# Ten sums of a codebook level go behind the block sums of the queries' stage

## The reference, cut to what matters

```python
def _L0_attn_ref(hidden_states, Wq, bq, Wk, bk, Wv, bv, Wo, bo, gq, gk):
    q = rms_norm(hidden_states @ Wq + bq, gq)      # 32 heads x 128, keys alike
    attn = softmax(einsum('bhqd,bhkd->bhqk', q, k) * scale)
    out = einsum('bhqk,bhkd->bhqd', attn, v)
    return out @ Wo + bo

def _L0_cond2_ref(x, weight, scale_log, codebook, lora_A, lora_B):
    lora_delta = lora_B @ lora_A * (LORA_ALPHA / LORA_RANK)
    cb = codebook / clip(max(abs(codebook)), 1e-08)
    normalized = (weight + lora_delta).reshape(O, I // GROUP, GROUP) / exp(scale_log)
    idx = searchsorted((cb[:-1] + cb[1:]) * 0.5, normalized, side='left')
    w = cb[idx] - normalized + normalized
    return x @ ((w * scale).reshape(O, I) + lora_delta).T
```

## Time and profile before

| what | value |
|---|---|
| median of 3 runs | 1450.33 us |
| the profiled execution | 1451.06 us |
| its span, first to last instruction | 1449.3 us |
| TensorE matmuls busy | 1444.4 us (100%) |
| TensorE weight loads busy | 1200.5 us (83%) |
| VectorE busy | 1080.4 us (75%) |
| ScalarE / GpSimd busy | 726.0 us (50%) / 745.2 us (51%) |
| granted TensorE clock | 1.000 |

### The profile page before, as it was taken

One profiled execution on the slowest core, in us unless ns is written; L12 is line 12 of the kernel. 1 busy time (PEld: TensorE's weight loads), 2 busy tenths in 40 slices (PEclk: granted clock), 3 DMA queues, 4 the chain that ended last, 5 costly groups with the idle time before them and its releaser, 6 DMA issues.

```text
span 1449.3 us, 34721 instructions
## 1 busy us (share of the span) xinstructions
PE 1444.4 (100%) x14507; PEld 1200.5 (83%) x14507; DVE 1080.4 (75%) x1507; ACT 726.0 (50%) x1331; POOL 745.2 (51%) x530
## 2 busy tenths in 40 slices
PE   9999999999999999999999999999999999999999
PEld 8788888888888888888888888888888888888887
DVE  8787868687786877875478888867987667667663
ACT  7766676766766767677333333334432322222221
POOL 7568777777777877776345555514561111112100
PEclk9999999999999999999999999999999999999999
DMA  4211011110111011102443344447663334244230
GB/s 152 66 45 45 31 38 45 45 45 24 45 45 45 27 41 45 45 31 67 136 152 139 133 133 137 145 148 246 201 194 110 103 118 132 83 137 132 74 118 30
DMA packets 106989, 135.13 MB, mean 93 GB/s; under 512 B 6224, under 2 KB 89424, under 8 KB 106320
## 3 DMA queue, kind: packets, MB, share of 16 engines
q1 hardware_dynamic: 106400, 132.62, 27.7%
q10 hardware_dynamic: 432, 0.30, 0.1%
HBM read 86.75 MB, written 46.14 MB: 92 GB/s over the span
## 4 chain that ended last, share of the span: by engine, by line
PE 98%; DVE 1%; issue 0%; ACT 0%; DVEq 0%; POOL 0%; ACTq 0%; POOLq 0%
PE bank L720 41%; PE bank L963 25%; PE bank L739 21%; PE bank L922 4%; PE bank L848 3%; PE bank L991 1%; PE bank L1009 1%; PE bank L669 0%; DVE wa L1623 0%; PE bank L648 0%; PE bank L977 0%; PE bank L1020 0%; DVE xs_lo L1685 0%; DVE sqst L1707 0%; PE bank L1041 0%
## 5 line engine op out<-in xcount | busy, mean ns | idle before, releaser
L720 PE MATMUL bank<-xs_hi,wa 128*128 128x512 f32 x1792 | 563.9, 392 | 0.0
L1526 POOL TENSOR_TENSOR accr<-accr,sqst 128x512 f32<-128x512 f32 x248 | 351.9, 1429 | 149.7 <-ACT sqst L1196 109.9
L720 PEld LDWEIGHTS bank<-xs_hi,wa 128*128 128x128 f32 x1792 | 336.3, 188 | 74.5 <-DVE qk L1774 2.4
L720 PE MATMUL bank<-xs_lo,wa 128*128 128x512 f32 x896 | 349.0, 390 | 0.0
L963 PE MATMUL bank<-ot,wo_main 128*128 128x512 f32 x1344 | 316.4, 392 | 0.0
L963 PEld LDWEIGHTS bank<-ot,wo_main 128*128 128x128 f32 x1344 | 249.6, 188 | 52.5
L739 PE MATMUL bank<-wv,xs_hi 128*128 128x512 f32 (+1 forms) x1008 | 282.6, 366 | 0.1
L1623 DVE TENSOR_TENSOR wa<-wraw,wa 128x256 fp32r<-128x256 f32 (+1 forms) x160 | 159.4, 997 | 96.2 <-ACT wa L1105 94.3
L1321 ACT ACTIVATE ot<-bank,vec 128x256 fp32r<-128x256 f32 x256 | 100.2, 475 | 240.4 <-PE bank L963 146.5
L739 PEld LDWEIGHTS bank<-wv,xs_hi 128*128 128x128 f32 x1008 | 182.1, 189 | 32.8 <-issue 1.9
L720 PEld LDWEIGHTS bank<-xs_lo,wa 128*128 128x128 f32 x896 | 168.3, 188 | 33.6
(11 more groups left out here) (224 smaller groups left out, 1724.5 us busy)
## 6 DMA issues: line engine op xcount, KB each, us to landing
values_b<-v_spill SPq DMA_DIRECT2D x60, 512.0 KB, 4.9
wraw<-in_wqk SPq DMA_DIRECT2D x32, 512.0 KB, 3.5
v_spill<-qk SPq DMA_DIRECT2D x64, 256.0 KB, 2.3
v_spill<-sqst SPq DMA_DIRECT2D x64, 256.0 KB, 2.1
score_spill<-sqst SPq DMA_DIRECT2D x32, 256.0 KB, 2.0
wraw<-in_wv SPq DMA_DIRECT2D x16, 512.0 KB, 5.1
wraw<-score_spill SPq DMA_DIRECT2D x16, 512.0 KB, 4.0
spare<-in_wo SPq DMA_DIRECT2D x15, 512.0 KB, 4.9
```

The lines of the kernel that those rows point to most:

```text
L720: ins = pe.matmul(dst[:, :], wa[:, col:col + P], xpart[:, j - 1, kt, n * CH:(n + 1) * CH], start=(first and k == 0), stop=(k == 5), skip_g ...
L1526: pool.tensor_tensor(a, a, sq_slot(count), ALU.add).then_inc(acc_done, 1)
```

## The change

In the ten instances s = 6 and s = 8, 14, 20, ..., 56 the level is taken apart: its comparison stays where it was, and its sum goes behind block_11(s+1), ahead of low_qk(1). In all other instances the order is as before.

```diff
+def level_split(s):
+    return s == 6 or 6 < s < 60 and s % 6 == 2
...
-            def level(half, t):
+            def level_step(half, t):
                 link(dve.tensor_scalar(qm, qv[half], thr[:, t + 1:t + 2], step[:, t:t + 1], ALU.is_gt, ALU.mult))
+
+            def level_sum(half):
                 link(dve.tensor_tensor(qf[half], qf[half], qm, ALU.add))
+
+            def level(half, t):
+                level_step(half, t)
+                level_sum(half)
...
                 if levels_qk(s):
-                    level(0, taken)
+                    level_step(0, taken)
                     taken += 1
+                    if not level_split(s):
+                        level_sum(0)
...
                 if s == 5:
                     code_order(NCODE // 16, 1)
+                if level_split(s):
+                    level_sum(0)
                 if levels_qk(s) == 2:
```

More of the change, by code:

```diff
@@ L1724, in first_level @@
                 link(dve.tensor_scalar(qf[half], qv[half], 0.0, cb[:, 0:1], ALU.mult, ALU.add))
+            def level_step(half, t):
+                link(dve.tensor_scalar(qm, qv[half], thr[:, t + 1:t + 2], step[:, t:t + 1], ALU.is_gt, ALU.mult))
+            def level_sum(half):
+                link(dve.tensor_tensor(qf[half], qf[half], qm, ALU.add))
             def level(half, t):
-                link(dve.tensor_scalar(qm, qv[half], thr[:, t + 1:t + 2], step[:, t:t + 1], ALU.is_gt, ALU.mult))
-                link(dve.tensor_tensor(qf[half], qf[half], qm, ALU.add))
+                level_step(half, t)
+                level_sum(half)
             def straight_through(half, steps=(0, 1)):
```

## The result

The changed kernel takes 1453.86 us (12 runs, 1453.09 to 1454.43), the kernel before on the same chips 1450.41 (12 runs). The ratio is 1.0023, with a 95% interval of 1.0015 to 1.0032: slower by 3.45 us. The forecast was 1449.4, and the time lies outside the range of 1448.7 to 1451.6. The case that came is the rival "block_12 comes too late", for which I gave 0.20 and 1452.1 us; the loss is nearly twice the 1.8 us that I had priced for it.

The account below looks back on a forecast made before the run. TensorE, busy nearly the whole span, was taken as the bound, so only its waits could be won: 0.81 in front plus 0.1 at s = 6, nothing behind, 1450.33 - 0.9 = 1449.4 us; range 1448.7 to 1451.6.

Parts of the forecast that it names:

- block_12 comes too late: Rival, moved sum to p3(s+1), s = 8 to 56: block_12 at 182.8 stalls 0.3 in each of nine, 1452.1; chance 0.20.
- Front gain, 0.81 us, the wait at p3(s) goes: Nine instances s = 8 to 56: without the sum in front, block_22 ends before p3's weight load wants it, 0.81 us won.
- Instance s = 6, 0.1 won: At s = 6 p3's 0.26 loss goes, but the next score block may wait longer; 0.1 us won overall.
- "bound" of zero: Lower end of the gain at s = 6, bounds 0 and 0.26 won: TensorE, coming earlier, may only wait longer.
- Behind, "I take 1.65 for the sum, the median of all 63", so "I cost it at nothing": Moved sum ahead of low_qk(1) and block_12(s): block_12 done at 181.8 to 182.6, within the slack, cost zero.
- The threshold and its price: At p3(s+1): stall begins when block_12 is done after about 182.5; every further 0.1 us costs 0.9 us in all.
- A rule against this change: Moved sum meets GpSimd's key-square adds; by the SBUF contention rule its long form is expected: no gain or the slower rival.
- The whole standstill is lost time: Rival, weight loads waiting for block_22: nothing of their 2.4 us is hidden, all comes back, 1447.9; chance 0.05.
- What would show it: Signs of being wrong: odd instances' p3 waits for block_22; sum over 2 us with low_qk(6) past 9.4; or nine keep 0.1.

Follow-up runs that it names:

- the sums left out: The ten sums not done at all, their comparisons kept, against the kernel before: 1449.71 against 1451.37 us, ratio 0.9989.
- the queries' adds short: Changed kernel with GpSimd's adds for q_hi(s) and q_lo(s+1) cut to 8 of 512 columns: 1449.47 against 1450.29 us of the kernel before, ratio 0.9994.
- next level put off: Changed kernel with the level of instances s % 6 == 3 moved behind block_11(s+1): 1453.17 against 1451.37 us of the kernel before, ratio 1.0013.

## Why the prediction was wrong

- *Front gain, 0.81 us, the wait at p3(s) goes:* right, a little high in size. No weight load waits for block_22(s) any more in the nine. With the sums left out their excess falls from 0.95 to between 0.3 and 0.4, so the gain is 0.6 rather than 0.81.
- *Instance s = 6, 0.1 won:* wrong. Its excess doubled, from 0.55 to 1.11. The "bound" of zero there was none. I had said that the chain hangs on block_12(6), which the moved sum does not make earlier, and did not ask whether it makes it later; it did. The load of p3(7) stands for 0.50 (0.41 at p3(6) before), and the score block at s = 8 waits 0.7 instead of 0.25.
- *Behind, "I take 1.65 for the sum, the median of all 63", so "I cost it at nothing":* this is the step that failed. The median says nothing of a place where the neighbour on GpSimd is known. I had listed both adds and even the rule that decides. The sum took 2.00 and low_qk(1), for which I kept one value, 1.67 and not 1.36. On the times of s = 14 before, block_12 is done at 175.71 + 7.12 = 182.8, 0.2 past my 181.8 to 182.6 and 0.3 past the threshold of 182.5. The rival priced exactly 182.8: 0.3 in each, 1452.1.
- *The threshold and its price:* near the mark. The wait came at p3(s+1), where it was named. block_12 is 1.23 late and block_22(15) 0.76, and p3(15) had about 0.35 of cover (12.15 less 11.80); the row of p3(15) grew by 0.34 where the rival had 0.3. The path was told in part only. I counted ScalarE's queue, and took low_qk(6) at its length of before. The run with the queries' adds short shows that this length hangs on GpSimd's pair of adds: with ScalarE's copy just as late and the adds gone, low_qk(6) takes 0.69 and nothing is lost at p3(s+1). How much of the 0.9 by which low_qk(6) starts later is ScalarE's copy and how much VectorE's own backlog is not settled: the copy landed at 10.06 behind the score block's end, VectorE was free at 10.25.
- *Why 3.45 and not the rival's 1.8:* s = 6 lost 0.56 instead of winning 0.1. The nine gained 0.6 in front and not 0.81. The rest is in the nine too, whose excess is 0.45 to 0.52 each where the rival had 0.3; the wait for low_qk(1) is one part of it that the prediction had no term for.
- *A rule against this change:* The Trainium skill, "SBUF — State Buffer", section "Who interferes with whom", had it right, including that who is issued first goes through and the other is blocked. The sum led by 0.23 and took 1.21, and trailed by 0.37 and took 2.00. Had it stood still until the add's end, 178.94 + 1.29 = 180.23, and then run for 1.21, it would have ended at 181.44; it ended at 181.31. I read the rule, wrote that the long form was to be expected by it, and then took the median.
- *The whole standstill is lost time:* no. In p3(15) the load stood for 0.49 and the two matmuls' row grew to 0.96, by 0.34 over 0.62; the hidden part is 0.15, near my 0.16. By the rule on overlap in the Trainium skill, "TensorE: Matmul & The Clock Gate", section "The mechanism", nothing would be hidden; the rows differ, and they decide. The same section names a second case in which a load is pulled ahead, that of the background weight buffer; I had left it out, and no run here shows which case this is.
- *What would show it:* of the signs of being wrong, the waits of odd instances for block_22 came, and a sum of 2.00 with low_qk(6) at 10.28, past 9.4.

One thing to read with care: the chain of waits in the changed kernel names ScalarE's copy of line 1170 as what released block_22(15).

```profile
187.42 0.58 ACT snap L1170
188.06 0.31 issue
188.37 0.69 DVE qk L1784
```

block_22 waits for the copy a3 (line 1188), not for line 1170, which is a1. What held it was low_qk(6) ahead of it in VectorE's order, 186.77 to 188.45. The run with the queries' adds short bears that out: there block_22(15) starts at 185.80, ahead of the copy a1, which starts at 185.87.

What stays open: at s = 6 the 1.11 came again (1.07 to 1.10 in three more traces that have the move there), but the 0.55 of before is told by one trace, and how the 1.11 is made up was not taken apart. The share of the wait for low_qk(1) is an estimate, and the 0.03 to 0.05 that the nine keep with the sums left out has no wait shown.

## What to carry to other kernels

Where two engines disturb each other, the duration of a moved operation is not its median but a matter of what runs on the other engine at its new start. Look up that neighbour's start, and whether the moved operation will lead or trail it. Try the places one by one, since one place here was worth 5 us of 1450. And follow a delay through to what it moves on the other engines: the loss was paid one instance later, behind operations that nobody had touched. When one of them is longer than before, look whether it fills what was an idle gap before you count it as a loss.

## What the runs showed of the hardware that I had not expected

The ordinary stretch of 84 matmuls is 19.28 to 19.29 in two traces (before, and next level put off) and 19.24 to 19.25 in the others. Over 29 stretches that is 1.2 us, a third of this result, with the granted clock at 1.0 in all. Its cause was not looked for; it is why excesses are taken within one trace. And a lead of a few hundredths decides who is slowed: the next sum led GpSimd's adds by 0.07 us before and took 1.23, and trailed them by 0.02 in the changed kernel and took 2.37.
